# DMA transposes of the attention probabilities replaced by TensorE transposes with copies on VectorE, in a transformer layer on eight cores

## The chip, the cores and the metric

The kernel runs on the eight cores of one Trainium2 chip, on two dies of four cores each. Every core computes 1024 of the 8192 tokens, with a halo of 64 tokens on either side, and no core sends anything to another. The metric is the device time of the slowest core, in microseconds (us). Lower is better.

## The reference

One layer on x of shape (2, 4096, 2048): a layer norm, a banded attention with learned sink keys, and a gated MLP whose output gates the attention's.

```python
x = L0_attn_u
xn = _layernorm(x, axis=-1)
s = _L0_attn_ref(xn, Wqkv, bqkv, Wo, bo, sinks)   # 32 heads of 64, rope, blocks of 64
g = _silu(_L0_ffn_ref(xn, w_gate_up, w_down))     # 2048 -> 8192 -> 2048
x = x + s * g
# inside the attention, for a block of queries and its three blocks of keys:
p = jax.nn.softmax(jnp.concatenate([s_sink, s_band], axis=-1), axis=-1)
O = jnp.einsum('bhnqs,hsd->bhnqd', p[..., :S], sinks) \
  + jnp.einsum('bhnqk,bhnkd->bhnqd', p[..., S:], Vband)      # S = 16 sink keys
```

## The kernel before

The work runs in stages with a barrier between them: the layer norm with transposes of x (to 95 us), a mixed stage of q/k/v projections and attention (123 to 1334 us), the MLP with the output projection, and a last stage that adds x and stores. The change lies in the mixed stage alone.

**Units.** The projections are cut into units of one PSUM buffer ps_qk (two buffers in turn). A q/k unit (L516) is 16 matmuls of 512 tokens; each chunk of two heads has two of them for q and two for k, and a fifth for the last 128 tokens of k. VectorE and ScalarE then apply the rope: VectorE multiplies the PSUM tile by the cosines (L620), ScalarE copies it in four pieces of 32 partitions with the halves swapped (L678 to L681), VectorE multiplies these by the sines (L624) and adds (L628). A v unit (L529, L532) is 16 matmuls of 256 columns and one for the bias, and ScalarE copies it out (L685). Even steps have nine v units, for four heads.

**Pairs.** A pair is one chunk of two heads (A and B) and one tile of 128 queries. There are 16 chunks x 8 tiles = 128 pairs. A pair passes through these pieces:

- scores on TensorE (L548 to L552): 128 queries x 272 keys, 16 sink keys and a band of 256, for A into psA and for B into psB, two buffers each;
- maxima on VectorE (L633, L634) and their scaling (L636, L637);
- exp on ScalarE (L693, L696) into pA_bf and pB_bf (three buffers, bf16), with the row sums;
- reciprocals and scaling of the probabilities on VectorE (L642 to L647);
- the transposes. The 16 sink columns of A and of B go through TensorE (L561, L562) into ps_tp, and VectorE copies them to pts_sb (L652, L653). The band, four blocks of 128x128, goes by four DMA transposes that SP issues (L727) into pt_sb;
- AV on TensorE (L578, L581, L584): six matmuls, three for each head, into the single ps_o;
- evacuation of ps_o by ScalarE in two halves (L662, L664). After the last tile of a chunk SP stores o_buf.

**Order.** A list written out by the host code interleaves units and pairs; each engine issues its own list in order. Step c computes the units of chunk c and the eight pairs of chunk c-1: unit, pair, unit, pair. Step 0 has no pairs, step 16 (the closing step) has pairs alone. So an odd step has five rounds with a q/k unit and a pair and three with a pair alone; an even step (2 to 14) has five rounds with a q/k unit, three with a v unit, and then six v units alone. For pair j TensorE's list has: scores of j, transposes of j-1, AV of j-3. VectorE's has: maxima of j, scaling of j, copies of j-1. ScalarE's has: exp of j, evacuation of j-3. After the pairs of a step the rest follows on TensorE: AV of pair 5, transposes of pair 7, AV of 6, AV of 7 (pairs counted from 0 within the step).

**Waits that matter.** TensorE's transposes of j wait until VectorE has scaled j and has copied j-1 out of ps_tp, of which there is one. AV of j waits for the copies of j, for the four DMA transposes of j, and for the evacuation of j-1. The exp of j waits for the maxima, and from pair 3 on for TensorE's transposes of j-3 and for the four DMA transposes of j-3, since they read the buffer that it overwrites. Each wait is an instruction of its own; the helper `wait` of `_PT` issues four. The weights of the units come by DMA from the GpSimd queue into three buffers wx, each load as soon as the unit that used the buffer three loads ago has ended.

## Time and profile before

| | us |
|---|---|
| median of 2 runs | 3002.68 |
| lowest, highest | 2994.1, 3011.26 |
| profiled execution | 3014.46 |
| its span, slowest core (core 5) | 3012.9 |
| spans of the eight cores | 2950.3 to 3012.9 |
| mean granted clock of TensorE, core 5 | 0.853 |

All rows below are of core 5 in the profiled execution. TensorE is busy for 80% of the span, VectorE for 26%, ScalarE for 18%. Over the mixed stage alone (120 to 1336 us) the granted clock of TensorE has a mean of 0.72, over the rest that follows 0.94. A granted clock of 1.00 stands for 2.4 GHz, 0.50 for 1.2 GHz.

In a row of a timeline stand: start in us, duration in us, engine, line, operation, output and inputs with shapes, how many were merged, and in brackets the idle time before it and what ended that. In a row of grouped instructions stand the busy time, the mean of one in ns, and the idle time before them. In a row of waits stand the engine and line that waited, what for, and the total, the number and the longest, in us. In a row of windows stand the stretch, its length, and for TensorE, its weight loads, VectorE, ScalarE and GpSimd the busy time with the number of instructions, then TensorE's mean granted clock, the DMA share and GB/s.

### The profile page before, as it was taken

The numbers are of one execution on the slowest core, as the hardware profiler recorded it, in microseconds if no ns is written. First come the engines' busy times: TensorE is split into PE (matmuls) and PEld (weight loads), VectorE is DVE, ScalarE is ACT, GpSimd is POOL, SyncE is SP. The second block draws the span as 40 slices with busy tenths as digits, with TensorE's granted clock in tenths as the row PEclk, the third lists the DMA queues.
The fourth block names the chain that finished last, engine by engine and source line by source line (L and its number), as shares of the span: only waits on it lengthen the run. The fifth ranks groups of instructions, "written<-read, shape, count | busy, mean of one in ns | idle before, by whom it ended". The sixth has DMA issues, their size and how long they took to land.

```text
span 3012.9 us, 33514 instructions; the slowest of 8 cores (2950.3 to 3012.9 us)
## 1 busy us (share of the span) xinstructions
PE 2399.1 (80%) x11224; PEld 1115.3 (37%) x11224; DVE 773.1 (26%) x2225; ACT 547.6 (18%) x1351; POOL 136.8 (5%) x259
## 2 busy tenths in 40 slices
PE   2476776767676768649999999999999999997775
PEld 1143333333333424214444444444444444442223
DVE  5233333333333333321211213121121312121114
ACT  4133333333333333320000000000000000000000
POOL 0000000000000000000001010000101010000000
PEclk9977777776777766659999999999999999998885
DMA  4421212121212121035627152453616144342226
GB/s 127 62 45 35 46 34 45 34 45 33 45 34 45 34 46 32 18 71 104 98 43 125 27 96 47 73 95 55 114 29 110 37 84 78 64 84 35 35 35 223
DMA packets 132675, 189.88 MB, mean 63 GB/s; under 512 B 92064, under 2 KB 93216, under 8 KB 128288
## 3 DMA queue, kind: packets, MB, share of 16 engines
q0 software_dynamic: 41616, 134.99, 26.7%
q1 hardware_dynamic: 90896, 52.75, 6.3%
q8 instruction: 98, 1.61, 0.2%
q14 instruction: 65, 0.53, 0.1%
HBM read 293.27 MB, written 12.58 MB: 102 GB/s over the span
## 4 chain that ended last, share of the span: by engine, by line
PE 56%; DMA 12%; DVE 9%; ACT 8%; SPq 6%; issue 5%; DVEq 1%; POOL 1%; ACTq 0%; POOLq 0%
PE ps_d L902 14%; PE ps_g L876 12%; PE ps_u L888 11%; DMA wd_ib<-wd_pack 6%; SPq L727 6%; PE ps_qk L529 5%; PE ps_s L917 5%; PE ps_qk L516 3%; DMA wobuf<-wo_pack 3%; DVE m L624 2%; DVE t L620 2%; ACT pB_bf L696 1%; ACT pA_bf L693 1%; ACT t2sw L681 1%; ACT t2sw L680 1%
## 5 line engine op out<-in xcount | busy, mean ns | idle before, releaser
L902 PE MATMUL ps_d<-h_ib,wd_ib 128*128 128x512 bf16 x2048 | 458.1, 386 | 39.5 <-DMA wd_ib<-wd_pack 39.5
L876 PE MATMUL ps_g<-xn_f,gbuf 128*128 128x512 bf16 x2048 | 465.3, 380 | 15.6 <-DMA gbuf<-wgu_pack 15.6
L888 PE MATMUL ps_u<-xn_f,ubuf 128*128 128x512 bf16 x2048 | 462.9, 379 | 0.0
L516 PE MATMUL ps_qk<-xn_f,wx 128*128 128x512 bf16 (+1 forms) x1280 | 330.0, 429 | 33.7 <-DMA wx<-wqkv_pack 27.8
L902 PEld LDWEIGHTS ps_d<-h_ib,wd_ib 128*128 128x128 bf16 x2048 | 202.9, 99 | 292.2 <-issue 59.6
L932 ACT ACTIVATE tg<-ps_g 128x512 f32<-128x512 f32 x128 | 76.5, 598 | 1239.9 <-PE ps_g L876 1239.8
L954 DVE TENSOR_TENSOR h_ib<-tg,ps_u 128x512 bf16<-128x512 f32 x128 | 88.0, 688 | 824.7 <-PE ps_u L888 824.7
L876 PEld LDWEIGHTS ps_g<-xn_f,gbuf 128*128 128x128 bf16 x2048 | 200.9, 98 | 259.0 <-issue 19.0
L888 PEld LDWEIGHTS ps_u<-xn_f,ubuf 128*128 128x128 bf16 x2048 | 200.4, 98 | 241.6
L964 DVE TENSOR_TENSOR g_sb<-g_sb,ps_d 128x512 f32<-128x512 f32 x224 | 154.0, 688 | 273.9 <-PE ps_d L902 273.9
L516 PEld LDWEIGHTS ps_qk<-xn_f,wx 128*128 128x128 bf16 x1280 | 136.7, 119 | 204.3 <-issue 132.7
L561 PE MATMUL ps_tp<-id_bf,pA_bf 128*16 128x128 bf16 x128 | 31.7, 248 | 222.2 <-DVE pts_sb L653 167.3
L917 PE MATMUL ps_s<-o_sb,wobuf 128*128 128x512 bf16 x512 | 143.4, 450 | 62.6 <-DMA wobuf<-wo_pack 62.6
L578 PE MATMUL ps_o<-pt_sb,v_t 128*64 128x128 bf16 x256 | 72.6, 284 | 134.4 <-DMA pt_sb<-pB_bf 93.8
L529 PE MATMUL ps_qk<-wx,xn_f 128*128 128x256 bf16 x1152 | 172.5, 315 | 4.0 <-DVE k_f L628 4.0
L693 ACT ACTIVATE pA_bf<-psA,smallp,consts_sb 128x272 bf16<-128x272 f32 x128 | 74.2, 579 | 350.7 <-DVE smallp L637 307.8
L529 PEld LDWEIGHTS ps_qk<-wx,xn_f 128*128 128x128 bf16 x1152 | 122.7, 112 | 38.9 <-issue 5.0
L917 PEld LDWEIGHTS ps_s<-o_sb,wobuf 128*128 128x128 bf16 x512 | 56.2, 112 | 149.6 <-issue 110.0
L620 DVE SCALAR_TENSOR_TENSOR t<-ps_qk,bq_pc,ck_t 128x512 f32<-128x512 f32 (+1 forms) x80 | 52.6, 658 | 224.0 <-PE ps_qk L516 223.5
L561 PEld LDWEIGHTS ps_tp<-id_bf,pA_bf 128*16 128x16 bf16 x128 | 11.1, 86 | 246.4 <-issue 243.7
L624 DVE SCALAR_TENSOR_TENSOR m<-t2sw,bq_sw,sk_t 128x512 f32<-128x512 f32 (+1 forms) x80 | 53.7, 671 | 187.4 <-ACT t2sw L681 187.4
L578 PEld LDWEIGHTS ps_o<-pt_sb,v_t 128*64 128x64 bf16 x256 | 31.2, 122 | 173.0 <-issue 158.2
(83 smaller groups left out, 1762.0 us busy)
## 6 DMA issues: line engine op xcount, KB each, us to landing
gbuf<-wgu_pack POOLq DMA_DIRECT2D x64, 512.0 KB, 6.2
ubuf<-wgu_pack POOLq DMA_DIRECT2D x64, 512.0 KB, 6.3
wd_ib<-wd_pack POOLq DMA_DIRECT2D x64, 512.0 KB, 18.2
wx<-wqkv_pack POOLq DMA_DIRECT2D x32, 512.0 KB, 5.2
u_all<-u_ext SPq DMA_DIRECT2D x9, 1024.0 KB, 17.8
wx<-v_pack POOLq DMA_DIRECT2D x8, 1024.0 KB, 9.1
wobuf<-wo_pack POOLq DMA_DIRECT2D x16, 512.0 KB, 5.1
u_buf<-u_ext SPq DMA_DIRECT2D x8, 1024.0 KB, 7.1
```

Source lines behind the costliest of these rows:

```text
L516: ins = t.matmul(p[:, 0:ln], w[:, kc * 128:(kc + 1) * 128], src[:, kc, :], start=(kc == 0), stop=(kc == 15))
L529: t.matmul(p[:, 0:256], xn_f[:, kc, tt * 128:(tt + 1) * 128], w[:, kc * 256:(kc + 1) * 256], start=(kc == 0), stop=False)
L578: t.matmul(outp, v_t[:, qt, h * 64:(h + 1) * 64], pt_sb[i % 3][:, co:co + 128], start=True, stop=False, tile_position=tp_)
L620: ctx.inc(v.scalar_tensor_tensor(t1[:, 0:ln], p[:, 0:ln], bq_pc[:, oc:oc + 1], cs, OP.add, OP.mult), "VS")
L624: v.scalar_tensor_tensor(m2[:, 0:ln], sw[:, 0:ln], bq_sw[:, oc:oc + 1], ss_, OP.add, OP.mult)
L693: sc.activation(pA_bf[j % 3][:], psA[j % 2][:], AF.Exp, bias=n2A[j % 3], scale=consts[:, 3:4], accum_out=rsA[j % 3])
L727: s.dma_start_transpose(dst[:, p * 128:(p + 1) * 128], srcs[p]).then_inc(PTp[p].sems[j % 3], 16)
L876: ins = t.matmul(pg[:], gbuf[ic % 2][:, kc * 128:(kc + 1) * 128], xn_f[:, kc, HALO + tsx * 512:HALO + (tsx + 1) * 512], start=(kc == 0), s ...
L888: ins = t.matmul(pu[:], ubuf[ic % 2][:, kc * 128:(kc + 1) * 128], xn_f[:, kc, HALO + tsx * 512:HALO + (tsx + 1) * 512], start=(kc == 0), s ...
L902: ins = t.matmul(pd[:], wd_ib[:, ic, oc * 128:(oc + 1) * 128], h_ib[:, ic, tsx * 512:(tsx + 1) * 512], start=(ic == 0), stop=(ic == 7))
L917: ins = t.matmul(pw[:], wobuf[0][:, kc * 128:(kc + 1) * 128], o_sb[:, kc, tw * 512:(tw + 1) * 512], start=(kc == 0), stop=(kc == 15))
L964: ins = v.tensor_add(dst, dst, ps_d[j % 2][:])
```

## The change

The four band blocks of a pair are transposed by TensorE, as the sink columns already were: six transposes per pair instead of two. ps_tp grows from 16 partitions x 256 columns to 128 x 768 (1536 bytes of each partition). VectorE copies the band blocks to pt_sb in two copies of 128 x 256 and the sink columns as before, so four copies per pair instead of two. SP issues no transposes any more, only the store of each chunk, and the waits for them on TensorE (AV) and on ScalarE (exp) are gone. Buffers, lists and all other counts stay.

```diff
--- before.py
+++ after.py
@@ -558,14 +558,17 @@
                     ctx.wait(t, "VS", vs_pt[i - 1])
                 pt = ps_tp
                 pa, pb = pA_bf[i % 3], pB_bf[i % 3]
-                t.transpose(pt[:, 0:128], pa[:, 0:NS], id_bf[:])
-                ins = t.transpose(pt[:, 128:256], pb[:, 0:NS], id_bf[:])
+                t.transpose(pt[:, 0:128], pa[:, NS:NS + 128], id_bf[:])
+                t.transpose(pt[:, 128:256], pa[:, NS + 128:NS + 256], id_bf[:])
+                t.transpose(pt[0:NS, 256:384], pa[:, 0:NS], id_bf[:])
+                t.transpose(pt[:, 384:512], pb[:, NS:NS + 128], id_bf[:])
+                t.transpose(pt[:, 512:640], pb[:, NS + 128:NS + 256], id_bf[:])
+                ins = t.transpose(pt[0:NS, 640:768], pb[:, 0:NS], id_bf[:])
                 ctx.inc(ins, "TS")
 
             def p3_emit_av(t, i):
                 c, qt = pairs[i]
                 ctx.wait(t, "VS", vs_pt[i])
-                PT.wait(t, pttok[i])
                 if i >= 1:
                     ctx.wait(t, "SS", ss_oe[i - 1])
                 vu = [u for u in unit_of_step[2 * (c // 2)] if u[0] == "v"][-1]
@@ -649,9 +652,11 @@
                     else:
                         j = x
                         ctx.wait(v, "TS", ts_tp[j])
-                        v.tensor_copy(pts_sb[j % 3][:, 0:128], ps_tp[:, 0:128])
+                        v.tensor_copy(pt_sb[j % 3][:, 0:256], ps_tp[:, 0:256])
+                        v.tensor_copy(pt_sb[j % 3][:, 256:512], ps_tp[:, 384:640])
+                        v.tensor_copy(pts_sb[j % 3][:, 0:128], ps_tp[0:NS, 256:384])
                         ctx.inc(v.tensor_copy(pts_sb[j % 3][:, 128:256],
-                                              ps_tp[:, 128:256]), "VS")
+                                              ps_tp[0:NS, 640:768]), "VS")
 
             def pm_scalar(sc):
                 def emit_oevac(i):
@@ -689,7 +694,6 @@
                         ctx.wait(sc, "VS", vs_mx[j])
                         if j >= 3:
                             ctx.wait(sc, "TS", ts_tp[j - 3])
-                            PT.wait(sc, pttok[j - 3])
                         sc.activation(pA_bf[j % 3][:], psA[j % 2][:], AF.Exp,
                                       bias=n2A[j % 3], scale=consts[:, 3:4],
                                       accum_out=rsA[j % 3])
@@ -700,37 +704,12 @@
                     else:
                         emit_oevac(x)
 
-            PTp = [Slots(nc, glob, f"pt{p}", 3) for p in range(4)]
-            pttok = [None] * NP3
-            ptc = [0, 0, 0]
-            for j in range(NP3):
-                ptc[j % 3] += 16
-                pttok[j] = (j % 3, ptc[j % 3])
-
-            class _PT:
-                def wait(self, eng, tok):
-                    for p in range(4):
-                        PTp[p].wait(eng, tok)
-            PT = _PT()
-
             def pm_sync(s):
-                for j in range(NP3):
-                    c, qt = pairs[j]
-                    ctx.wait(s, "VS", vs_nm[j])
-                    if j >= 3:
-                        ctx.wait(s, "TS", ts_av[j - 3])
-                    pa, pb = pA_bf[j % 3], pB_bf[j % 3]
-                    dst = pt_sb[j % 3]
-                    srcs = [pa[:, NS:NS + 128], pa[:, NS + 128:NS + 256],
-                            pb[:, NS:NS + 128], pb[:, NS + 128:NS + 256]]
-                    for p in range(4):
-                        s.dma_start_transpose(dst[:, p * 128:(p + 1) * 128],
-                                              srcs[p]).then_inc(PTp[p].sems[j % 3], 16)
-                        PTp[p].cnt[j % 3] += 16
-                    if qt == NT_OWN - 1:
-                        ctx.wait(s, "SS", ss_oe[j])
-                        tok = OS.dma(s, d_oscr[c], o_buf[c % 2][:], c % 2)
-                        assert tok == ostok[c]
+                for c in range(16):
+                    last_i = c * NT_OWN + (NT_OWN - 1)
+                    ctx.wait(s, "SS", ss_oe[last_i])
+                    tok = OS.dma(s, d_oscr[c], o_buf[c % 2][:], c % 2)
+                    assert tok == ostok[c]
 
             with ExitStack() as sPM:
                 ps_qk = [sPM.enter_context(nc.psum_tensor(f"ps_qk{i}", [128, 512], F32))
@@ -739,7 +718,7 @@
                        for i in range(2)]
                 psB = [sPM.enter_context(nc.psum_tensor(f"psB{i}", [128, 272], F32))
                        for i in range(2)]
-                ps_tp = sPM.enter_context(nc.psum_tensor("ps_tp", [NS, 256], BF16))
+                ps_tp = sPM.enter_context(nc.psum_tensor("ps_tp", [128, 768], BF16))
                 ps_o = sPM.enter_context(nc.psum_tensor("ps_o", [128, 128], F32))
                 block.tensor(pm_tensor)
                 block.vector(pm_vector)
```

## Rows read from the trace of the kernel before

**Rows 1.** Windows: one odd step (chunk 7), and the closing step.

```profile
614.10:684.80 70.70, 42.54 (x194) 18.39 (x194) 25.18 (x95) 23.87 (x68) 1.06 (x2) 0.67 0.22 43
1283.60:1333.00 49.40, 24.01 (x113) 9.78 (x112) 15.61 (x80) 13.98 (x49) 0.00 (x0) 0.50 0.12 27
```

**Rows 2.** Waits of all engines, 120 to 1336 us.

```profile
DVE m L624 <- ACT t2sw L681: 187.4, 80, 3.8
...
PE ps_o L578 <- DMA pt_sb<-pB_bf: 93.8, 30, 3.9
```

**Rows 3.** Timeline of an odd step's end: SP, VectorE, TensorE.

```profile
661.40 3.10 SPq L727 DMA_TRANSPOSE pt_sb<-pA_bf  x2
...
672.74 0.20 DVE L653 COPY pts_sb<-ps_tp 16x128 bf16<-16x128 bf16 x1
...
683.56 0.28 PE L578 MATMUL ps_o<-pt_sb,v_t 128*64 128x128 bf16 x1 [3.90 <-DMA pt_sb<-pB_bf]
...
684.72 5.11 PE L516 MATMUL ps_qk<-xn_f,wx 128*128 128x512 bf16 x16
```

**Rows 4.** Groups by shape: VectorE operations in the three main stages.

```profile
L636 DVE TENSOR_TENSOR smallp<-smallp,consts_sb 128x1 f32<-128x1 f32 x128 | 20.4, 159 | 10.3 <-issue 0.9
...
L246 DVE COPY xn_f<-ps_tr 128x128 bf16<-128x128 bf16 x144 | 25.8, 220 | 29.9 <-PE ps_tr L218 29.9
...
L962 DVE COPY g_sb<-ps_d 128x512 f32<-128x512 f32 x32 | 22.1, 691 | 42.5 <-PE ps_d L902 42.5
```

**Rows 5.** Timeline of the closing step: VectorE's maxima, last AV matmul.

```profile
1289.03 0.43 DVE L633 TENSOR_REDUCE smallp<-psA 128x1 f32<-128x272 f32 x1
...
1289.38 0.43 DVE L634 TENSOR_REDUCE smallp<-psB 128x1 f32<-128x272 f32 x1
...
1292.79 0.42 DVE L633 TENSOR_REDUCE smallp<-psA 128x1 f32<-128x272 f32 x1
...
1332.59 0.31 PE L584 MATMUL ps_o<-pts_sb,sinkn_bf 16*64 16x128 bf16 x1
```

**Rows 6.** Timeline, TensorE: first matmul of an AV group, and the unit behind it.

```profile
717.06 0.29 PE L578 MATMUL ps_o<-pt_sb,v_t 128*64 128x128 bf16 x1 [0.48 <-issue]
...
718.22 1.89 PE L516 MATMUL ps_qk<-xn_f,wx 128*128 128x128 bf16 x16
```

**Rows 7.** Timeline, VectorE: reciprocals of pairs 2 and 3 of the first odd step.

```profile
200.29 0.16 DVE L642 RECIPROCAL smallp<-smallp 128x1 f32<-128x1 f32 x1 [1.43 <-ACT pB_bf L696]
...
209.40 0.16 DVE L642 RECIPROCAL smallp<-smallp 128x1 f32<-128x1 f32 x1 [1.70 <-ACT pB_bf L696]
```

**Rows 8.** Timeline, TensorE: a 512-column unit and the transposes behind it.

```profile
699.13 6.41 PE L516 MATMUL ps_qk<-xn_f,wx 128*128 128x512 bf16 x16
...
707.44 0.22 PE L561 MATMUL ps_tp<-id_bf,pA_bf 128*16 128x128 bf16 x1 [0.94 <-DVE pts_sb L653]
```

**Rows 9.** Timeline, TensorE: transposes in a round without a unit.

```profile
665.42 0.26 PE L561 MATMUL ps_tp<-id_bf,pA_bf 128*16 128x128 bf16 x1 [0.17 <-DVE pts_sb L653]
```

**Rows 10.** Timeline, TensorE: last AV group of an even step.

```profile
314.85 0.22 PE L578 MATMUL ps_o<-pt_sb,v_t 128*64 128x128 bf16 x1 [0.93 <-ACT o_buf L664]
```

**Rows 11.** Timeline, TensorE: v units of two rounds that follow each other.

```profile
726.93 3.59 PE L529 MATMUL ps_qk<-wx,xn_f 128*128 128x256 bf16 x16
...
733.70 3.59 PE L529 MATMUL ps_qk<-wx,xn_f 128*128 128x256 bf16 x16
```

**Rows 12.** Windows: v parts of the seven even steps with pairs; two, and the sum.

```profile
282.70:311.20 28.50, 27.26 (x196) 18.68 (x195) 8.20 (x41) 9.70 (x32) 0.00 (x0) 0.90 0.11 23
...
726.90:762.10 35.20, 35.20 (x196) 21.27 (x195) 8.16 (x41) 9.71 (x32) 0.00 (x0) 0.63 0.09 19
...
sum 217.30, PE 212.35 PEld 137.55 DVE 57.14 ACT 67.95 POOL 0.00; mean PE 30.34 PEld 19.65 DVE 8.16 ACT 9.71 POOL 0.00
```

**Rows 13.** Windows in the first stage: before TensorE's first transpose, and among them.

```profile
35.00:40.00 5.00, 0.00 (x0) 0.00 (x0) 3.69 (x9) 2.21 (x3) 0.00 (x0) 1.00 0.00 0
...
85.00:90.00 5.00, 2.69 (x14) 1.36 (x13) 2.43 (x14) 1.02 (x1) 0.00 (x0) 1.00 0.00 0
```

## The prediction

> **What bounds the kernel now.** I read first the windows cut at the steps of the mixed stage [rows 1]. An odd step (five q/k units, eight pairs) takes 70.7 us with TensorE busy for 42.5; the closing step, eight pairs alone, takes 49.4 with no engine busy for more than half. So I went to the waits of the stage [rows 2]: TensorE waits 93.8 us, 30 times, at L578 for a DMA transpose, and VectorE 187.4 us at L624 for ScalarE's copies. The second means that the round of a q/k unit is one serial path which passes between VectorE and ScalarE; the first is the wait that the change takes away.
>
> The end of an odd step, in order of time, shows where [rows 3]. Pair 4 is normalised at 661.3; from 661.40 SP issues the 16 transposes of pairs 4 to 7, and the last lands for the L578 of 683.56, after 3.90 us of waiting: (683.2 - 661.4) / 16 = 1.36 us each, 5.4 a pair. VectorE had copied pair 6 by 672.74 + 0.20 = 672.9. The next step starts at 684.72. In rounds with a unit a pair comes every 8.5 us and SP keeps up; it is late only where pairs stand alone, at the ends of the eight odd steps and in the closing one.
>
> **What the change costs and gives, part by part.**
>
> *Copies on VectorE.* Each pair gets two copies of 128x256 bf16 from PSUM, a shape that no row has. A one-column operation takes 159 ns, 128 columns of bf16 from PSUM 220, 512 columns of f32 from PSUM 691 [rows 4]: 61 ns for 128 columns against 532 for 512, so bf16 flows about twice as fast as f32. I estimate 159 + 122 = 0.28 us. Of two passes without a wait the second starts about 0.08 before the first ends (L633, 0.43 us long, and L634 0.35 later [rows 5]), so one copy takes 0.20 us of the path and two 0.40. Bounds: no less than two 128-column copies, 2 x 0.14 = 0.28; no more than two 272-column f32 passes, 2 x 0.35 = 0.70. I take 0.40: the bf16 row is the nearer.
>
> *Transposes on TensorE.* Four more per pair, with 128x128 weights. The nearest row is the 128-column unit, 16 matmuls with such weights in 1.89 us, 0.118 each at the lower clock (1.2 GHz); the dearest are the six matmuls of an AV group, 717.06 to 718.22, 0.19 each [rows 6]. So 0.47 us per pair, at most 0.77. I take 0.47: same shape, back to back.
>
> *Waits on ScalarE.* The exp of pair j waits also for the four transposes of pair j-3, by four wait instructions behind the one on VectorE, all long met. They are not free. Pairs 0 to 2 have neither these nor the wait on TensorE: VectorE idles 1.43 us for the exps of pair 2 and 1.70 for those of pair 3 [rows 7]. 0.27 us for five waits is 0.054 each, 0.22 for the four that go. The exp is on the serial path, so each pair gives 0.22 back; the bounds are 0 (TensorE's wait alone costs the 0.27) and 0.27.
>
> *Waits on TensorE.* Four go from the AV group as well. Where TensorE has a gap between L562 and L578 (about 0.4 us), the sequencer passes these waits there; with six transposes in flight it passes the rest of them meanwhile. There I count 0.2 for the transposes instead of 0.47; where TensorE is busy throughout, the full 0.47.
>
> *SP.* 512 issues go and 16 stores stay. The transposes' bytes hid under other work and give nothing else back.
>
> *Round with a q/k unit.* VectorE copies pair j-1 at the end of round j, on the path: +0.40 - 0.22 = +0.18. The transposes lie beside it: before L561 TensorE waits at least 0.94 us in such rounds [rows 8]. If that cover were gone, a round would cost 0.47 more.
>
> *Round without one.* It takes VectorE and ScalarE 3.76 us (L633 of 1289.03 to that of 1292.79 [rows 5]), now 3.94. TensorE has little cover here, it waits only 0.17 us for the copies [rows 9]: 3.8 + 0.2 = 4.0 if it sets the pace. I take 3.98.
>
> *Odd step.* Until pair 6 is copied there are seven pairs' copies and eight pairs' exps: 7 x 0.40 - 8 x 0.22 = +1.0, with 0.1 for TensorE's pace 672.9 becomes 674.0. Then comes the chain that was hidden: pair 7's transposes 0.15 + 0.77 (0.31 now), to 674.9; AV 6 1.2, to 676.1; ScalarE's evacuation of the single ps_o with both hand-overs 1.0, to 677.1; AV 7 1.2, to 678.3. What is late next is this evacuation; another step shows the same chain without a DMA in it, TensorE waiting 0.93 for L664 [rows 10]. Pair 7's copies end by 676.1 and hide under AV 6. Gain 684.7 - 678.3 = 6.4.
>
> *Even step* (seven with pairs; nine v units more). SP is not late here. Before the first v unit lie three pairs' copies and four pairs' exps, 1.2 - 0.88 = +0.3, and one set of transposes, 0.2. Three rounds have a pair and a v unit; in this one TensorE paces them without a gap, 6.77 us each [rows 11]: 3 x 0.47 = 1.4. The last transposes hide in the wait for L664. Loss 1.9.
>
> *Closing step.* 1289.03 - 0.22 + 7 x 3.98 = 1316.7; the odd step's end chain (674.0 to 678.3) 4.3, so 1321.0 against 1332.8 now [rows 5]. Gain 11.8. The store and the first MLP load behind it stay.
>
> **Sum.** 8 x 6.4 = 51.2, 0.7 less for the three pairs that never had the waits, + 11.8 - 7 x 1.9 = 13.3: 49 gained. The profiled execution took 3014.5 us (span 3012.9), of which 2965 would be left. The median of the two runs shown is 3002.7, so I forecast 2954.
>
> Copies at 0.70: 0.30 x (7 x 8 + 3 x 7 + 7 = 84) = 25 less. At 0.28, only rounds that VectorE paces gain, 0.12 x 53 = 6 more. Transposes at 0.77: 0.30 x (21 v rounds + 31 rounds without a unit + 7) = 18 less. Waits worth nothing: 0.22 x (64 + 28 + 8 = 100) = 22 less.
>
> *The clock* has no price of its own in the rows of the change. The v part of an even step took 28.5 us at a granted clock of 0.90 in one step and 35.2 at 0.63 in another; the seven sum to 217.3, mean 31.0 [rows 12]. The changed rounds have another length and other matmuls. All seven fast: 18 us less; all slow: 29 more.
>
> **Rivals.**
> 1. *Copies or transposes at their upper bounds*: 2979 or 2972, both 2997. For it: both prices come from other shapes. Against: the rows nearest in type and in weights.
> 2. *The waits give nothing back*, since the sequencer passes them while ScalarE is idle: 2976. Against: they stand behind the one that is met last, and the step from 1.43 to 1.70 comes with the first pair that has them.
> 3. *The clock falls and the kernel gets slower.* All v parts slow: 2983. If every 512-column unit runs at the lower clock too, a unit round holds 6.4 (L516 at 699.13 [rows 8]) + 1.4 for scores (6.77 less 3.9 for the v unit, 1.2 for AV, 0.3) + 0.8 + 1.2 + 0.3 = 10.1 on TensorE against 8.65 on the serial path, and three such rounds in 15 steps cost 1.45 more each: 65, together 3048. It decides once TensorE's work in a round passes 8.65, a unit of 4.9 us in every round. Against: L516 of 699.13 was at the lower clock, yet TensorE still waited 0.94 behind it.
>    The Trainium skill (TensorE: Matmul & The Clock Gate, Part 4: PE-mode transpose) says that transposes do not count as the activity that raises the clock. By that rule the v parts would all be slow, 2983. The trace does not decide it: before the stage TensorE did nothing but transposes, 2.69 of 5 us, at a granted clock of 1.00, but the clock was 1.00 before the first of them too [rows 13].
> 4. *The clock rises*, since the near idleness at the odd ends and in the closing step (granted clock 0.50 [rows 1]) shrinks: v parts all fast 2936; with units at step starts 1.4 us shorter, 15 of them, 2915. Against: rounds of 4 us still leave TensorE gaps.
>
> **How the numbers follow.** Forecast 0.50 (own range 2940 to 2972), upper costs 0.18, waits worthless 0.10, clock down 0.08, clock up 0.14. The range 2925 to 2992 reaches from between the two fast clock cases to nearly both costs high. 2% is 60 us, about what can be told from no change here; below 2943 lie 0.10 of the forecast and 0.13 of the clock-up case: faster 0.23. Slower by 2%, beyond 3062, needs the clock down and high costs: 0.02. Within: 0.75.
>
> **What would show it.** Odd steps of about 64 us, a closing step of about 38, even ones up by 2. No wait of L578 on a DMA, and TensorE's last waits of a step on L664. Copies of 0.28 us. VectorE's wait before L642 at 1.48 for all pairs. Unit rounds of 8.65 us. I am wrong if the copies take 0.43, if that wait stays at 1.70, if the v parts sum far from 227, or if odd steps stay near 70 us, which would mean that another wait has taken the place of SP's.

## The result, and the profile after

| | before | after |
|---|---|---|
| median, us | 3032.57 | 2952.71 |
| lowest, us | 2994.1 | 2921.78 |
| profiled execution, us | 3014.46 | 2960.48 |
| its span, slowest core, us | 3012.9 (core 5) | 2959.0 (core 1) |
| mean span of the eight cores, us | 2979.3 | 2928.7 |
| after / before | | 0.980, 95% interval 0.975 to 0.985 |

The medians are over ten executions of before and eleven of after, disturbed ones among them, which the ratio leaves out: the undisturbed ones alone have medians near 3000 and 2945 us. The forecast was 2954 us in a range of 2925 to 2992, 49 us less than before. By the ratio the change is worth 2.0%, about 60 us; the interval leaves open on which side of 2% it lies.

The windows of core 1 are those that answer to [rows 1]: an odd step (chunk 7), and the closing step, here from its first scores to the evacuation of the last pair.

```profile
593.30:657.70 64.40, 46.59 (x225) 20.59 (x224) 28.34 (x111) 24.22 (x68) 1.06 (x2) 0.69 0.17 33
...
1230.70:1268.50 37.80, 29.73 (x145) 12.43 (x144) 18.65 (x96) 14.20 (x49) 0.00 (x0) 0.50 0.02 8
```

The odd step fell from 70.7 to 64.4 us, the closing step from 49.4 to 37.8. The same between two events, the starts of VectorE's first maxima and of ScalarE's evacuation of the last pair. Before, 47.8 us:

```profile
1285.24 0.44 DVE L633 TENSOR_REDUCE smallp<-psA 128x1 f32<-128x272 f32 x1 [10.73 <-PE psB L552]
...
1333.00 0.27 ACT L662 ACTIVATE o_buf<-ps_o 64x128 bf16<-64x128 f32 x1 [4.42 <-PE ps_o L584]
```

After, 36.2 us, 11.5 less:

```profile
1232.28 0.44 DVE L636 TENSOR_REDUCE smallp<-psA 128x1 f32<-128x272 f32 x1 [4.00 <-PE psB L552]
...
1268.49 0.27 ACT L667 ACTIVATE o_buf<-ps_o 64x128 bf16<-64x128 f32 x1 [1.57 <-PE ps_o L587]
```

The waits of the stage (120 to 1336 us), which answer to [rows 2], no longer hold one of the AV group (now L581) on a DMA; its last wait is for the evacuation, and VectorE's wait for the rope copies is as it was:

```profile
DVE m L627 <- ACT t2sw L686: 187.8, 80, 3.8
...
PE ps_o L581 <- ACT o_buf L669: 23.0, 26, 0.9
```

The end of that odd step, in order of time, answers to [rows 3]:

```profile
651.34 0.16 DVE L645 RECIPROCAL smallp<-smallp 128x1 f32<-128x1 f32 x1 [1.48 <-ACT pB_bf L700]
...
652.20 0.28 PE L581 MATMUL ps_o<-pt_sb,v_t 128*64 128x128 bf16 x1 [0.90 <-ACT o_buf L669]
...
652.58 0.20 DVE L658 COPY pts_sb<-ps_tp 16x128 bf16<-16x128 bf16 x1
...
653.36 0.29 PE L561 MATMUL ps_tp<-id_bf,pA_bf 128*128 128x128 bf16 x1
...
654.42 0.32 PE L581 MATMUL ps_o<-pt_sb,v_t 128*64 128x128 bf16 x1
...
656.58 0.28 PE L581 MATMUL ps_o<-pt_sb,v_t 128*64 128x128 bf16 x1 [0.90 <-ACT o_buf L669]
...
657.73 1.89 PE L516 MATMUL ps_qk<-xn_f,wx 128*128 128x512 bf16 x4
```

From the copies of pair 6 (end 652.78) to the next step it takes 4.95 us, where it took 11.8. The groups of VectorE show its wait for the exps before, 220.1 / 127 = 1.73 us a pair (first row), and after the new copies and that wait, 190.3 / 128 = 1.49:

```profile
L642 DVE RECIPROCAL smallp<-smallp 128x1 f32<-128x1 f32 x128 | 20.9, 164 | 222.1 <-ACT pB_bf L696 220.1 <-ACT o_buf L664 2.1
...
L655 DVE COPY pt_sb<-ps_tp 128x256 bf16<-128x256 bf16 x128 | 36.5, 285 | 95.2 <-PE ps_tp L566 95.2
...
L645 DVE RECIPROCAL smallp<-smallp 128x1 f32<-128x1 f32 x128 | 21.0, 164 | 190.3 <-ACT pB_bf L700 190.3
```

**Parts of the stage, all cores.** One core's step hangs on where its clock stands, so I also took the starts of the steps and of the maxima from the traces of all eight cores and formed means, in us. "Odd" and "even" are whole steps, "v part" runs from the first v unit of an even step to the end of the last, "end" is the last odd step with the closing one, "stage" the first unit to the first MLP load, "rest" what follows.

| | odd | even | v part | even less v part | end | stage | rest |
|---|---|---|---|---|---|---|---|
| before | 70.1 | 77.8 | 30.7 | 47.1 | 122.6 | 1205.6 | 1652.0 |
| after | 63.7 | 78.5 | 30.7 | 47.8 | 104.7 | 1148.4 | 1657.9 |

And the rounds of the odd steps, from one pair's maxima to the next pair's (four rounds with a unit, the last a short one, then three without; "to first" is from the step's start, its first unit, to the first maxima, "tail" from the last maxima to the next step):

| | to first | rounds with a unit | without | tail |
|---|---|---|---|---|
| before | 10.36 | 8.43, 8.72, 8.78, 6.37 | 3.77, 3.89, 3.81 | 15.94 |
| after | 9.85 | 8.23, 9.02, 9.08, 6.50 | 3.94, 4.05, 3.94 | 9.04 |

The stage lost 57.2 us: 7 x 6.4 in odd steps, 17.9 at the end, 7 x 0.7 given back in even ones, and 0.8 in step 0. The rest took 5.8 more in these two executions; over all the kernels below it lies between 1633 and 1661 with the same code, so that is no effect of the change.

The odd steps are not quite free of the clock. In "to first" the time from the end of the first unit to the first maxima is 5.07 us before and after; the unit itself fell from 5.29 to 4.78 us in the mean, at a mean granted clock of 0.69 and then 0.76. So 0.5 of the 6.4 us is clock, and 5.9 the rounds and the tail. The first round, which has no copies yet and only loses the waits on ScalarE, fell from 8.43 to 8.23, by the 0.20 that those waits were said to cost.

**The v rounds.** A v round, one with a pair and a v unit, is paced by TensorE at the lower clock, and here the forecast's price of the transposes can be read. At the full clock, the kernel before:

```profile
296.73 0.28 DVE L647 TENSOR_SCALAR pB_bf<-pB_bf,smallp 128x272 bf16<-128x272 bf16 x1
...
297.41 0.22 PE L561 MATMUL ps_tp<-id_bf,pA_bf 128*16 128x128 bf16 x1
297.46 0.22 PE L562 MATMUL ps_tp<-id_bf,pB_bf 128*16 128x128 bf16 x1
298.17 0.22 PE L578 MATMUL ps_o<-pt_sb,v_t 128*64 128x128 bf16 x1 [0.49 <-issue]
```

The first row ends the scaling, at 297.01, of the pair whose transposes follow. And the changed kernel:

```profile
431.85 0.23 PE L561 MATMUL ps_tp<-id_bf,pA_bf 128*128 128x128 bf16 x1
431.92 0.22 PE L562 MATMUL ps_tp<-id_bf,pA_bf 128*128 128x128 bf16 x1
432.07 0.22 PE L563 MATMUL ps_tp<-id_bf,pA_bf 128*16 128x128 bf16 x1
432.22 0.23 PE L564 MATMUL ps_tp<-id_bf,pB_bf 128*128 128x128 bf16 x1
432.29 0.22 PE L565 MATMUL ps_tp<-id_bf,pB_bf 128*128 128x128 bf16 x1
432.44 0.22 PE L566 MATMUL ps_tp<-id_bf,pB_bf 128*16 128x128 bf16 x1
432.59 0.24 PE L581 MATMUL ps_o<-pt_sb,v_t 128*64 128x128 bf16 x1
```

Two transposes with four waits behind them took 0.76 us, six without waits take 0.74: at the full clock the change is free there, and the v rounds of all cores that took under 5.2 us went from a median of 4.69 to one of 4.57 (means 4.61 and 4.63). At the lower clock they went from the 6.77 of [rows 11] to 7.52 (v units at 701.25, 708.77, 716.29). There the waits had cost nothing before, the AV group began 0.24 us behind L562, so nothing is won back and the four transposes cost 0.75.

### The profile page after: what moved, and what is told of

Read it like the earlier page. It is cut to its first block, busy times and chain, and to the rows that moved or that the text cites. A ratio compares the mean times of both kernels' runs of the same rounds, so it can differ in the third digit from the quotient of the medians.

```text
span 2959.0 us, 33017 instructions; the slowest of 8 cores (2884.4 to 2959.0 us)
## 1 busy us (share of the span) xinstructions
PE 2460.9 (83%) x11736; PEld 1146.2 (39%) x11736; DVE 823.6 (28%) x2481; ACT 550.3 (19%) x1351; POOL 136.8 (5%) x259
## 4 chain that ended last, share of the span: by engine, by line
PE 60%; DMA 13%; DVE 11%; ACT 9%; issue 5%; DVEq 1%; POOL 1%; SPq 0%; ACTq 0%; POOLq 0%
PE ps_d L881 15%; PE ps_g L855 11%; PE ps_u L867 11%; DMA wd_ib<-wd_pack 8%; PE ps_qk L529 5%; PE ps_s L896 5%; PE ps_qk L516 4%; DMA wobuf<-wo_pack 3%; ACT pA_bf L697 2%; ACT pB_bf L700 2%; DVE m L627 1%; PE ps_o L581 1%; DVE t L623 1%; PE ps_o L587 1%; ACT t2sw L686 1%
## 5 line engine op out<-in xcount | busy, mean ns | idle before, releaser
L516 PE MATMUL ps_qk<-xn_f,wx 128*128 128x512 bf16 (+1 forms) x1280 | 325.9, 423 | 29.7 <-DMA wx<-wqkv_pack 24.9
L561 PE MATMUL ps_tp<-id_bf,pA_bf 128*128 128x128 bf16 x128 | 32.1, 251 | 209.0 <-DVE pts_sb L658 158.4
L529 PE MATMUL ps_qk<-wx,xn_f 128*128 128x256 bf16 x1152 | 163.8, 304 | 4.0 <-DVE k_f L631 4.0
L561 PEld LDWEIGHTS ps_tp<-id_bf,pA_bf 128*128 128x128 bf16 x128 | 12.9, 101 | 232.5 <-issue 229.3
L581 PE MATMUL ps_o<-pt_sb,v_t 128*64 128x128 bf16 x256 | 73.7, 288 | 24.0 <-ACT o_buf L669 23.0
L37 POOL DMA_DIRECT2D gbuf<-wgu_pack x64 | 33.9, 530 | 1182.0 <-PE ps_g L855 1034.4
```

Source lines behind the costliest of these rows:

```text
L516: ins = t.matmul(p[:, 0:ln], w[:, kc * 128:(kc + 1) * 128], src[:, kc, :], start=(kc == 0), stop=(kc == 15))
L529: t.matmul(p[:, 0:256], xn_f[:, kc, tt * 128:(tt + 1) * 128], w[:, kc * 256:(kc + 1) * 256], start=(kc == 0), stop=False)
L581: t.matmul(outp, v_t[:, qt, h * 64:(h + 1) * 64], pt_sb[i % 3][:, co:co + 128], start=True, stop=False, tile_position=tp_)
```

## The experiments

Each kernel is the one after with one edit, unless it says before. The edits are shown in part; lines that only widen a tile, rename a slot or adapt a count are left out, as are the new places of the transposes in e7 and the copies that go with them in e9. The same parts for all of them (means over eight cores of one profiled execution each, us):

| | odd | v part | even less v part | end | stage | ratio to before, 95% |
|---|---|---|---|---|---|---|
| e1_act_waits | 65.8 | 28.0 | 48.8 | 107.7 | 1153.4 | 0.985, 0.981 to 0.989 |
| e2_copies_twice | 66.2 | 29.0 | 49.1 | 109.3 | 1167.9 | 0.983, 0.980 to 0.987 |
| e3_two_more_transposes | 64.8 | 29.9 | 48.0 | 106.5 | 1152.9 | 0.982, 0.979 to 0.984 |
| e4_two_more_matmuls | 64.8 | 29.8 | 48.0 | 106.4 | 1152.1 | 0.981, 0.977 to 0.986 |
| e5_before_one_wait | 68.7 | 26.8 | 45.9 | 120.0 | 1158.2 | 0.986, 0.980 to 0.992 |
| e6_copies_under_exp | 61.4 | 27.8 | 46.3 | 100.7 | 1097.4 | 0.958, 0.954 to 0.963 |
| e7_two_copies | 62.7 | 29.7 | 46.9 | 102.1 | 1124.9 | 0.973, 0.968 to 0.978 |
| e8_both | 59.9 | 27.2 | 45.7 | 98.4 | 1075.9 | 0.952, 0.946 to 0.958 |
| e9_half_by_dma | 63.2 | 28.5 | 47.4 | 103.8 | 1125.4 | 0.971, 0.960 to 0.982 |
| e10_before_copies_under_exp | 69.1 | 28.4 | 46.4 | 121.4 | 1176.4 | none given |
| e11_half_under_exp | 61.1 | 26.9 | 46.3 | 100.5 | 1089.0 | 0.963, 0.947 to 0.979 |
| e12_sinks_last | 63.1 | 28.2 | 47.7 | 102.0 | 1122.2 | 0.970, 0.963 to 0.977 |

Only e6 and e8 stand clearly apart from the changed kernel by the ratio, whose own interval is 0.975 to 0.985; those of e7, e11 and e12 overlap it, and e1 to e5 and e9 can't be told from it. What an edit does is therefore read from the parts. Of e2 I use only the differences of single rounds: in its profile cores 4 to 7 had a mean granted clock of 0.850, cores 0 to 3 one of 0.867, and its v part and stage hold some of that. The rounds are the same to 0.01 us on both. e10 has no ratio, since its whole times lie too far apart (2957.22 to 3256.55 us).

**What do met waits cost ScalarE?** (rival 2) A wait is called met when what it waits for has long happened.

```diff
                         if j >= 3:
-                            ctx.wait(sc, "TS", ts_tp[j - 3])
+                            for _r in range(5):
+                                ctx.wait(sc, "TS", ts_tp[j - 3])
```

> The changed kernel with four waits put back ahead of each exp on ScalarE, on a TensorE count that is long met. Nothing else changes. Theory (a met wait behind the last one costs 0.054 us and lies on the serial path of VectorE and ScalarE): VectorE's idle time before its reciprocals (L645 and following) goes from 1.48 to 1.70 us for all pairs but the first three, odd steps go from 63.7 to 65.4 us (eight exps x 0.22), the whole by about 20 us, to 0.987 of the kernel before. Rival (the sequencer passes met waits while ScalarE is idle anyway): 1.48 us stays, odd steps stay at 63.7, ratio 0.98.

VectorE's wait for the exps:

```profile
L645 DVE RECIPROCAL smallp<-smallp 128x1 f32<-128x1 f32 x128 | 21.0, 164 | 219.5 <-ACT pB_bf L701 219.5
```

219.5 / 128 = 1.715 against 1.487: 0.228 for four waits, 0.057 each, and 1.73 was the value before. The rounds without a unit took 4.16, 4.18 and 4.14 where they took 3.94, 4.05 and 3.94. Rival 2 falls: waits that are long met cost what the prediction said where they stand behind the one that is met last. The odd steps grew by 2.1, 0.4 more than expected: "to first" grew by 0.7, which is the clock of the first unit again (5.50 us for 4.78), and the rest by 1.4. The stage grew by only 5.0 us, since the v parts came out 2.7 us shorter, of which more below.

**And the same from the other side:** the kernel before, its four transposes counted on one semaphore.

```diff
-            PTp = [Slots(nc, glob, f"pt{p}", 3) for p in range(4)]
+            PTp = [Slots(nc, glob, "pt", 3)]
-                    for p in range(4):
-                        PTp[p].wait(eng, tok)
+                    PTp[0].wait(eng, tok)
```

> The kernel before, with the four DMA transposes of a pair counting on one semaphore, so that one wait takes the place of four on ScalarE and on TensorE. Theory: 0.16 us less per exp on the serial path, VectorE's idle time before L642 from 1.72 (220 us in 128) to 1.56; but SP still ends the odd steps, so an odd step gains only what starts its last transposes earlier, five exps, 0.8 us (70.1 to 69.3), the closing step nothing, an even step 0.6: 11 us in all, ratio 0.996. Rival (the waits are the larger part of the whole gain): odd steps gain 1.3 or more, ratio 0.99 or less. Third (they cost nothing): no change.

```profile
L642 DVE RECIPROCAL smallp<-smallp 128x1 f32<-128x1 f32 x128 | 21.0, 164 | 200.1 <-ACT pB_bf L696 198.3 <-ACT o_buf L664 1.9
...
PE ps_o L578 <- DMA pt_sb<-pB_bf: 99.6, 30, 4.6
```

The first row is a group of VectorE, the second a wait of TensorE. Three waits fewer bring the wait for the exps to 198.3 / 127 = 1.56, 0.17 less, and leave TensorE's wait for DMA at the odd ends where it was: the two terms are separate.

The odd steps gained 1.3 us and the ratio is 0.986. That is what the rival asked for, and not the 0.8 and 0.996 of the theory. Its seven rounds gave 7 x 0.17 = 1.2 as they should; another 0.45 is in "to first", where the first unit took 4.84 us for 5.29, and the tail took back 0.3. It doesn't follow that the waits are the larger part of the change: 27 us of this kernel's 47 in the stage lie in its v parts (7 x 3.9), shorter rounds and a better clock together, and the closing pairs still wait for SP.

Three waits went from TensorE too. The AV group follows VectorE's scaling sooner:

```profile
290.41 0.29 DVE L647 TENSOR_SCALAR pB_bf<-pB_bf,smallp 128x272 bf16<-128x272 bf16 x1
...
291.14 0.22 PE L561 MATMUL ps_tp<-id_bf,pA_bf 128*16 128x128 bf16 x1
...
291.54 0.22 PE L578 MATMUL ps_o<-pt_sb,v_t 128*64 128x128 bf16 x1
```

From the end of L647 to L578 it is 0.84 us here and 1.16 before (297.01 to 298.17); over the v rounds of all cores these are the shortest times in each kernel, and at the full clock the most frequent. So three waits cost 0.32, 0.11 each. This v round took 4.20 us where 4.69 was usual before; of the 0.49, 0.32 are the waits on TensorE and 0.17 those on ScalarE, since the scaling ends that much earlier. They cost this only where the scaling ends shortly before the transposes. Where it ends earlier, four waits are free, as in a round of e10 below (the kernel before with another order, all four waits in place), where the AV group starts 0.15 us behind L562:

```profile
869.97 0.29 DVE L647 TENSOR_SCALAR pB_bf<-pB_bf,smallp 128x272 bf16<-128x272 bf16 x1
...
871.33 0.22 PE L562 MATMUL ps_tp<-id_bf,pB_bf 128*16 128x128 bf16 x1
...
871.48 0.24 PE L578 MATMUL ps_o<-pt_sb,v_t 128*64 128x128 bf16 x1
```

**What do the copies cost?**

```diff
+                        v.tensor_copy(mb[:, 0:256], ps_tp[:, 0:256])
+                        v.tensor_copy(mb[:, 256:512], ps_tp[:, 384:640])
                         v.tensor_copy(pt_sb[j % 3][:, 0:256], ps_tp[:, 0:256])
```

(mb is the work tile m2 read as bf16; the extra copies go unused.)

> The changed kernel with the two copies of 128x256 done a second time, into a buffer of the rope that is free then; the second result is not used. Theory (each of these copies costs 0.20 us of the serial path): 0.40 us more per pair wherever VectorE sets the pace, odd steps from 63.7 to 66.5 or 66.9 us (seven or eight pairs), even steps up by 1.2 to 2, in all about 34 us, ratio 0.991. Rival (part of it is hidden under ScalarE or TensorE): under half of that.

The rounds without a unit grew to 4.39, 4.34 and 4.32 us, by 0.45, 0.29 and 0.38: 0.37 in the mean for two copies, near the forecast's 0.40. In the trace of the changed kernel they start 0.20 us apart. The other way, in two copies for four (the sinks last, side by side in ps_tp):

```diff
-                        v.tensor_copy(pt_sb[j % 3][:, 0:256], ps_tp[:, 0:256])
-                        v.tensor_copy(pt_sb[j % 3][:, 256:512], ps_tp[:, 384:640])
-                        v.tensor_copy(pts_sb[j % 3][:, 0:128], ps_tp[0:NS, 256:384])
+                        v.tensor_copy(pt_sb[j % 3][:, 0:512], ps_tp[:, 0:512])
-                                              ps_tp[0:NS, 640:768]), "VS")
+                                              ps_tp[0:NS, 512:768]), "VS")
```

> The changed kernel with the six transposes laid out so that two copies do the work of four: one of 128x512 and one of 16x256. Theory: the same columns but two starts less, 0.07 us each, 0.14 per pair: odd steps 63.7 to 62.7, even ones 0.4 less before their v part, 12 us in all, ratio 0.976. Rival (a wider copy does not flow at two columns for one): no gain, the wide copy longer than 0.48 us.

```profile
L655 DVE COPY pt_sb<-ps_tp 128x512 bf16<-128x512 bf16 x128 | 53.6, 419 | 91.2 <-PE ps_tp L566 91.2
...
L656 DVE COPY pts_sb<-ps_tp 16x256 bf16<-16x256 bf16 x128 | 34.4, 269 | 0.0
```

419 ns for 512 columns where two of 256 took 285 and 282. The odd steps lost the 1.0 us expected. The edit also changed the order of the transposes, and e12 below shows how much of this is order.

**Does the kind of work on TensorE move its clock?** (rival 3) Two kernels with two more operations of the same shape per pair, whose results go unused: transposes, and plain matmuls.

```diff
+                t.transpose(pt[:, 768:896], pa[:, NS:NS + 128], id_bf[:])
+                t.transpose(pt[:, 896:1024], pb[:, NS:NS + 128], id_bf[:])
```
```diff
+                px = pt[:, 768:1024].bitcast(F32)
+                t.matmul(px, pa[:, NS:NS + 128], id_bf[:], start=True, stop=False)
+                t.matmul(px, pb[:, NS:NS + 128], id_bf[:], start=False, stop=True)
```

> The changed kernel with two more transposes of 128x128 per pair, ahead of the six, into unused columns of ps_tp; the results are not used. Theory: each costs TensorE 0.19 us at the lower clock, so a round with a v unit goes from 7.52 to 7.90 us there, a round without a unit grows by up to 0.38, unit rounds do not change; odd steps by 1 us, even ones by about 1.1, in all 15 to 20 us. Rival (transposes do not count as work that holds the clock up): the v parts of even steps, now 30.7 us on average, go toward 36, and the kernel loses over 40 us.

> As the kernel with two more transposes, but the two are ordinary matmuls with the same weights and the same moving operand, summed into f32 columns that nobody reads. Theory (the kind does not matter): the same time within 0.3%, the same v parts within 1 us. Rival (only ordinary matmuls hold the clock up): the v parts run at a higher granted clock than with transposes, 2 us or more less in each even step, 15 us or more in all.

The same even and odd step of core 3, first with transposes, then with matmuls (windows; the last three figures are the granted clock, the DMA share and GB/s):

```profile
521.30:600.10 78.80, 65.44 (x394) 36.06 (x393) 28.54 (x111) 27.36 (x77) 1.59 (x3) 0.82 0.12 23
600.10:665.10 65.00, 49.41 (x241) 22.49 (x240) 28.36 (x111) 24.17 (x68) 1.06 (x2) 0.66 0.16 31
```
```profile
515.80:594.60 78.80, 65.44 (x394) 36.03 (x393) 28.55 (x111) 27.36 (x77) 1.59 (x3) 0.82 0.12 23
594.60:659.60 65.00, 49.43 (x242) 22.52 (x242) 28.37 (x111) 24.17 (x68) 1.06 (x2) 0.66 0.16 31
```

They agree to the hundredth in clock and length, and in the table to 0.1 us, but for the stage (0.8). The rule of the Trainium skill that the prediction weighed (TensorE: Matmul & The Clock Gate, Part 4: PE-mode transpose), that transposes do not count as the activity that raises the clock, would have let the kernel with matmuls have the higher clock. It has not, so the pair shows no sign of the rule. It does not refute it either: both kernels have a mean granted clock of 0.87 in their v parts where the changed one has 0.82, and whether two plain matmuls can move it at all is not shown.

The prediction's own row on this point says nothing. It read a granted clock of 1.00 among the transposes of the first stage [rows 13], but the clock has no record there: on the eight cores the first one comes between 121.6 and 129.1 us, at 128.0 on core 5, and until then 1.00 stands in its place. The stage's first matmuls of 512 columns show it:

```profile
123.50:127.90 4.40, 4.40 (x11) 1.56 (x12) 0.00 (x0) 0.00 (x0) 0.00 (x0) 1.00 0.23 48
128.10:132.30 4.20, 4.20 (x21) 1.90 (x20) 0.75 (x1) 2.06 (x3) 0.00 (x0) 1.00 0.03 6
```

Eleven in 4.40 us are the pace of the lower clock (0.43 us from start to start), twenty-one in 4.20 that of the full one (0.22), and both rows say 1.00.

The two extra ones also gave a price that I had not expected: v rounds of 7.73 instead of 7.52 at the lower clock and 4.68 instead of 4.57 at the full one, 0.1 and 0.05 us each, while the four of the change had cost 0.75 / 4 = 0.19 at the lower. The two stand first, ahead of another band block. In the rows at 431.85 above, the starts of the transposes stand 0.07 us apart within the band, and 0.15 wherever a band block of 128 columns and a sink block of 16 follow each other, or an AV matmul of 64. So, with the order alone:

```diff
-                t.transpose(pt[0:NS, 256:384], pa[:, 0:NS], id_bf[:])
                 t.transpose(pt[:, 384:512], pb[:, NS:NS + 128], id_bf[:])
                 t.transpose(pt[:, 512:640], pb[:, NS + 128:NS + 256], id_bf[:])
+                t.transpose(pt[0:NS, 256:384], pa[:, 0:NS], id_bf[:])
                 ins = t.transpose(pt[0:NS, 640:768], pb[:, 0:NS], id_bf[:])
```

> The changed kernel with one thing altered: the order of its six transposes, the four band blocks first and then the two sink blocks of 16 columns, where the changed kernel has band, band, sink, band, band, sink. The copies stay four. In the changed kernel the starts of the six stand 0.06, 0.24, 0.21, 0.08, 0.25 us apart at the lower clock (1.04 us from L561 to L581); in e7_two_copies and e8_both, which have the sinks last, 0.82. Theory: each change between a band and a sink block costs about 0.1 us at the lower clock and 0.07 at the full one, and this, not the number of transposes, is why four more cost 0.75 us a v round instead of the 0.47 of the forecast. Then v rounds fall from 7.52 to about 7.30 us at the lower clock and from 4.57 to about 4.36 at the full one; odd steps, which VectorE and ScalarE pace, only from 63.7 to 63.5; so 0.8 of the 1.0 us that e7_two_copies took off an odd step are its copies. The whole kernel 0.978, 0.2% below the changed kernel, within what the v parts' clock does. Rival: the 0.82 came with the two copies and not with the order, v rounds stay at 7.52 and 4.57.

```profile
420.63 0.29 PE L561 MATMUL ps_tp<-id_bf,pA_bf 128*128 128x128 bf16 x1
420.71 0.31 PE L562 MATMUL ps_tp<-id_bf,pA_bf 128*128 128x128 bf16 x1
420.82 0.31 PE L563 MATMUL ps_tp<-id_bf,pB_bf 128*128 128x128 bf16 x1
420.92 0.31 PE L564 MATMUL ps_tp<-id_bf,pB_bf 128*128 128x128 bf16 x1
421.17 0.27 PE L565 MATMUL ps_tp<-id_bf,pA_bf 128*16 128x128 bf16 x1
421.24 0.31 PE L566 MATMUL ps_tp<-id_bf,pB_bf 128*16 128x128 bf16 x1
421.48 0.32 PE L581 MATMUL ps_o<-pt_sb,v_t 128*64 128x128 bf16 x1
```

0.85 us at the lower clock instead of 1.06; v rounds of 7.31 and 4.36, as in e7 and e8, which have this order too. Odd steps lost 0.5 rather than the 0.2 expected: 0.3 of it in the tail, where the last transposes stand on the path. So up to 0.5 of the 1.0 of e7 was order, and the rest its copies. The ratio is 0.970 where that of the changed kernel is 0.980, the intervals just overlapping; two thirds of the stage's 26 us come from the v parts (7 x 2.5), by 0.2 us a round and by the clock.

**Was it SP's rate, or DMA transposes as such?** The kernel before with head A's two blocks by DMA and head B's by TensorE:

```diff
+                t.transpose(pt[:, 128:256], pb[:, NS:NS + 128], id_bf[:])
+                t.transpose(pt[:, 256:384], pb[:, NS + 128:NS + 256], id_bf[:])
-                    srcs = [pa[:, NS:NS + 128], pa[:, NS + 128:NS + 256],
-                            pb[:, NS:NS + 128], pb[:, NS + 128:NS + 256]]
-                    for p in range(4):
+                    srcs = [pa[:, NS:NS + 128], pa[:, NS + 128:NS + 256]]
+                    for p in range(2):
```

> Head B transposed by TensorE and copied as in the changed kernel, head A by two DMA transposes as before. SP then needs 2.6 us per pair, less than a round without a unit takes. Theory (SP's rate was the trouble, not the DMA's way): no queue at the odd ends, one copy less (0.20) and two waits more (0.11) per pair on the path, pair 7 lands 0.8 us later than by TensorE: odd steps near 64, v parts' rounds 0.37 shorter, ratio 0.98, as the changed kernel. Rival (any DMA transpose in the chain costs its latency at each end): odd steps at 66 or more, ratio 0.985 or more.

Among TensorE's waits of the stage the DMA is all but gone, 2.8 us where it was 93.8, and the evacuation is the usual last one:

```profile
PE ps_o L580 <- ACT o_buf L667: 25.2, 30, 1.3
...
PE ps_o L580 <- DMA pt_sb<-pA_bf: 2.8, 2, 1.7
```

With two transposes a pair, SP needs 2.7 us (half of the 5.4) in rounds of 3.9 and keeps up; odd steps of 63.2 and an end of 103.8 are as short as with none. It was SP's rate, and a DMA transpose in the chain costs no latency that shows at the ends.

**Can the copies be hidden?** VectorE idles 1.49 us for the exps of each pair. The copies of pair j-1 need only TensorE's transposes of j-1, which are done by then:

```diff
                         vsched.append(("mx", j))
-                        vsched.append(("nm", j))
                         if j - 1 >= w0:
                             vsched.append(("ev", j - 1))
+                        vsched.append(("nm", j))
```

> The changed kernel with VectorE's copies of pair j-1 ahead of the scaling of pair j instead of behind it, so that they run while ScalarE computes the exps (VectorE idles 1.48 us there, the four copies take 0.67). Theory (the copies are on the serial path now): a unit round loses 0.67 us, a round without a unit 0.3 (TensorE's 3.65 us then set its pace), odd steps from 63.7 to 60.1, even steps 2.0 less before their v part, the closing step 2 less; 45 us in all, ratio 0.965. Rival (the transposes come too late for that place, so VectorE waits there for TensorE and delays the scaling): no gain or a loss in rounds without a unit. The v parts can add or take 20 us by their clock.

```profile
L645 DVE RECIPROCAL smallp<-smallp 128x1 f32<-128x1 f32 x128 | 21.0, 164 | 107.5 <-ACT pB_bf L700 107.5
...
684.91 0.44 DVE L636 TENSOR_REDUCE smallp<-psA 128x1 f32<-128x272 f32 x1 [1.20 <-PE psB L552]
```

The wait fell to 107.5 / 128 = 0.84, so 0.65 us of copies a pair left the path. Odd steps gained 2.3 and not 3.6: the middle rounds with a unit fell by 0.65 (9.02 to 8.38, 9.08 to 8.43), but of the three without, one stayed above 4 us (3.32, 4.16, 3.68), since TensorE paces it now, and "to first" grew by 0.7, by the clock of the first unit; without that the gain would be 3.0. In the v rounds VectorE now waits 1.20 us for the scores, as the second row (a timeline) shows. All seven v parts of core 6 take 27.5 to 28.0 us at a granted clock of 0.93 to 0.95. It beats both kernels, at 0.958 of the one before.

The same order in the kernel before:

> The kernel before, with only VectorE's order changed: the two sink copies of pair j-1 ahead of the normalisation of j, under its exps. It tells how much of the 4.2% of e6_copies_under_exp comes from the order alone. Theory (SP is what holds the ends of odd steps and the closing step): 0.28 us a pair leave VectorE's path, its wait before L642 falls from 1.73 to 1.45; an odd step gets 5 x 0.28 = 1.4 shorter, down to pair 4, from where SP's 16 transposes take their 21.8 us as before: 68.7; an even step without its v part 1.1 shorter, 46.0; the closing step, which SP paces from pair 0, stays within 0.3 us; TensorE's waits at L578 for a DMA stay above 90 us, 30 times. That is 20 us, ratio 0.993; by the v parts' clock, which came out better in five of seven runs with another round length, down to 0.98. Rival: the order is what matters and the DMA transposes would have done as well: odd steps near 62, stage near 1100 us, ratio near 0.96.

Odd steps lost 1.0, the wait on the DMA stayed (93.7 us, 30 times), and the stage lost 29, 16 of it in v parts (7 x 2.3). The order alone is not what makes e6: with SP's rate in the way most of it can't be had.

Both improvements together:

> The changed kernel with both improvements: VectorE copies pair j-1 before it normalises pair j, so under the exps of j, and in two copies (128x512 and 16x256) instead of four. Theory: the copies lie wholly under VectorE's wait for the exps (0.84 us of it is left in e6_copies_under_exp), so making them 0.12 us shorter only makes that wait longer, to about 0.96 us at L643, and buys nothing: odd steps 61.4, even steps without their v part 46.3, ratio about 0.958, as e6_copies_under_exp. Rival: TensorE sets the pace of the rounds without a unit once the copies are hidden, and ps_tp free earlier by 0.12 us lets it go on earlier: odd steps 61.0 and the closing step 0.8 shorter, ratio about 0.955. Against both: the gain of the two copies, 1.0 us an odd step, adds up in full, odd steps 60.4, ratio about 0.946.

```profile
L645 DVE RECIPROCAL smallp<-smallp 128x1 f32<-128x1 f32 x128 | 21.0, 164 | 126.7 <-ACT pB_bf L698 125.4 <-ACT o_buf L667 1.3
```

The wait grew to 125.4 / 127 = 0.99, as foreseen for copies that are hidden, and rounds with a unit stayed near 8.4. The odd steps, which the theory left at 61.4, came to 59.9 all the same, below all three forecasts. But the rounds that TensorE paces fell by 0.2 us (4.16 and 3.68 to 3.96 and 3.48; v rounds 4.57 to 4.36). I had written that ps_tp is free earlier; e12, run later, shows the same 0.2 with the four copies left, so it is the order of the transposes. Of the 1.5 us, 0.9 are in "to first" (9.67 for 10.56), where nothing but the first unit varies, so most of it is clock. The ratio of 0.952 is the lowest of all, though its interval overlaps that of e6.

And e6 on e9 (head A by DMA, copies under the exps):

> Head A's two band blocks by DMA transposes and head B's by TensorE, as e9_half_by_dma, and VectorE copies pair j-1 under the exps of j, as e6_copies_under_exp. In e6_copies_under_exp and e8_both TensorE paces the rounds without a unit (4.57 and 4.37 us, VectorE waits 1.2 and 1.0 us for the scores there). Theory: two transposes fewer on TensorE, 0.19 us each, take 0.38 off such a round, about 4.2 us, so odd steps come to 59.9 (e8_both 59.9, e6_copies_under_exp 61.4); even steps without their v part 45.7; VectorE's wait before L644 falls from 1.60 by the copies' 0.50 to 1.10; no wait on a DMA at L580; ratio about 0.952, the same as e8_both. Rival: with shorter rounds SP's two transposes a pair, 2.7 us, and their landing come last again: odd steps 63 as in e9_half_by_dma, waits of L580 on a DMA, ratio 0.965.

VectorE's wait came to 148.6 / 128 = 1.16, and AV groups waited for a DMA only twice, 3.0 us in all, but odd steps stayed at 61.1 where 59.9 was expected: with two transposes fewer than e8 on TensorE in each pair, its rounds without a unit (3.43, 3.85, 3.52) gained nothing on e8's (3.29, 3.96, 3.48), while ScalarE again passes two waits a pair, and rounds with a unit are 0.1 longer. Of the 1.2 us to e8, 0.5 are in "to first" (10.19 for 9.67), the first unit's clock, and 0.3 in the tail. Nothing is won over e8.

## Why the prediction came out

| step of the prediction | forecast | measured |
|---|---|---|
| odd step | -6.4 | -6.4 |
| closing step | -11.8 | -11.5 |
| even step | +1.9 | +0.7 |
| band copy: duration, start to start | 0.28, 0.20 | 0.285, 0.20 |
| VectorE's wait for the exps | 1.70 to 1.48 | 1.73 to 1.49 |
| round with a unit | +0.18, 8.65 | +0.13 in the mean, 9.0 in the middle ones |
| round without a unit | 3.76 to 3.98 | 3.82 to 3.98 |
| chain from pair 6's copies to the next step | 11.8 to 4.3 | 11.8 to 4.95 |
| four more transposes where TensorE is full | 0.47 | 0.75 at the lower clock, -0.1 with the waits at the full one |
| v parts of one core, sum | 227 | 217.6; mean of all cores 214.8, before 215.0 |
| whole stage | -49 | -57.2 |

**The bound** was named rightly: the changed rounds have no DMA wait, the last waits of a step are on the evacuation, and e9 shows that it was SP's rate and not its kind of transfer. The terms on the critical path had the right sign and place; what follows is about their size.

**The copies and the waits on ScalarE** were sized to a few hundredths, from rows of other shapes and from the one place where a pair with the waits stood beside one without. e1 and e2 each moved one of the two alone and found its price; e5 and e7 agree, though each moved a second thing with it (the waits on TensorE, the order of the transposes).

**The mis-sized term** is that of the transposes on TensorE, "0.47 us per pair, at most 0.77 ... same shape, back to back". They are not of one shape: two of six have 16 columns of weights, and the starts are 0.15 us apart at each change of shape and 0.07 within one (0.21 to 0.25 and 0.06 to 0.11 at the lower clock). In a round as in [rows 11] they cost 0.75, the upper bound. The end chain came out 0.65 longer than forecast as well: 1.06 for the transposes instead of 0.77, and 0.58 instead of 0.15 before them, in which the AV group of pair 5 still ran, itself late by the evacuation before it. That was offset in the odd step by rounds that grew less and a first one that began 0.5 earlier, by the clock of the step's first unit. That the odd step came out at -6.4 to the tenth is therefore partly luck, two errors of 0.6 that cancel.

**The second error is its mirror:** "waits on TensorE ... where TensorE is busy throughout, the full 0.47". At the full clock TensorE is not busy throughout in a v round before; it stands 0.49 us at the four waits between L562 and L578, and they went. There the change is 0.12 us faster in the median and even in the mean, not 0.47 slower. The even steps came out at +0.7 instead of +1.9 since the v rounds are of both kinds. That is 7 x 1.2 = 8 us, what the stage gained beyond the forecast (57 against 49). How many v rounds fall at the lower clock the prediction could not say, and with another share of them the even steps would have come out otherwise.

**The whole.** 2954 forecast and a median of 2952.71 agree better than the account does. From the base of 3002.7 the ratio gives 2943, 11 below the forecast and well inside its range; that the two figures come within 1.3 us is luck.

**The rivals.** Upper costs: for the transposes half right, as told, and worth less than forecast. Waits worthless: refuted by e1 and e5. Clock down: refuted for this change, the v parts are 30.7 us before and after, at a mean granted clock of 0.81 and 0.82; the rule that it leaned on stays open. Clock up: not in the v parts, but the first units of odd steps got 0.5 us shorter by it, 1.4 had been priced, while those of even steps got 0.3 longer (5.35 to 5.64); and much of e5, e6, e8 and e12 lives on it.

**What stays open** is what decides the clock of a v part. A v round costs 2.9 us more at the lower clock (7.52 - 4.57), and a v part differs by how many of its rounds fall there. Two v parts of one core of e12, with the same work:

```profile
408.00:441.40 33.40, 33.40 (x209) 20.86 (x209) 9.68 (x49) 9.71 (x32) 0.00 (x0) 0.71 0.00 1
554.30:581.20 26.90, 26.72 (x209) 18.57 (x208) 9.67 (x49) 9.70 (x32) 0.00 (x0) 0.95 0.01 2
```

Adding four waits (e1) brought the mean from 30.7 to 28.0, two transposes to 29.9, taking copies off the path 27.8: longer and shorter rounds alike. So I can't say that any of these edits "raises the clock"; each only shifts where the rounds stand. It puts some 20 us on the whole of any change to this stage that no count of instructions foretells, and is why I judged the edits by odd steps and by even steps less their v part. These are not wholly free of it, as the first unit shows; the single rounds are the safer measure.

## What to carry to other kernels

Ask of each queue what it needs per round, and compare that with the shortest round, not with the mean: SP's 5.4 us a pair were hidden in rounds of 8.5 and set the pace in rounds of 3.8. A wait that has long been met is not free where it stands behind the last one of a serial path; on a TensorE that has work queued it was free. Turning an order so that work falls under another engine's time was worth about as much here as the change itself (0.958 against 0.980); counting four transfers on one semaphore gave 0.986, more than half of that in v parts, where the clock has its share. Price a group of small matmuls from rows with the same sequence of shapes, and put like shapes side by side.
